# Attention in a cross-attention and mixture-of-experts block: the softmax sums and their reciprocal at the front of the pipeline step

## The chip, the core and the metric

The kernel runs on one core of a Trainium2 chip. The metric is the device time of one execution in microseconds. A core has a matrix engine (TensorE, PE in the profile), a vector engine (VectorE, DVE), an engine for activations (ScalarE, ACT), a general one (GpSimd, POOL), and queues that start transfers (SyncE, SP). Each engine works through its own instructions in order; semaphores tie the engines together. TensorE writes its results to PSUM, eight banks of 512 float32 for each of 128 partitions.

## The reference

Two parts, one after the other, on x of 2 x 2048 x 512 and a context of 2 x 128 x 512:

```
x = x + attention(layernorm(x), ctx, ctx, mask) @ W_out.T     # 16 heads of 32, 128 keys
x = x + experts(layernorm(x))                                 # 6 experts, the best 2 of each row
attention: energy = q.k, masked keys -1e20; attn = softmax(energy / sqrt(512)); out = attn.v
```

The change touches only how the softmax is divided by its sum: out = (sum over keys of exp(e) v) / (sum over keys of exp(e)).

## The kernel before

Attention is a software pipeline, written out by hand. A unit is four heads (a group g) of a block of 512 query rows: 8 blocks by 4 groups are 32 units (`ntile`). The loop `attention_loop` calls the function `attention(s)` of every engine for s = -2 to 43; step s does different stages of different units, each behind by its lag: `L_STAT` 0 (layer norm of a tile of 128 rows), `L_XT` 1 (its transposes), `L_TOK` 5 (scores by token, for the maxima), `L_MT` 9 (the maxima transposed, once for each block), `L_KEY` 10 (scores by key), `L_PV` 11 (sums, and products with the values), `L_DIV` 12 (division). What an engine does within a step is the order of the code; nothing else schedules it. All steps from 12 to 31 have every stage; step 33 and later have no tile to transpose, step 37 and later have no scores by token, the last scores by key are in step 41.

Each unit goes through these:

- Scores by token, in two pairs of heads (`scores_by_token`, pair 0 and 1; tok0 and tok1 in the prediction; the product in line 1350). Both pairs write the same two banks, `B_MX` and the next. VectorE takes the maximum over the keys (`maxima`, line 969), two reduces for each pair. Pair 1 waits for the reduces of pair 0 (`mx_done`).
- The maxima, negated and split in two by GpSimd (lines 662 and 665), are transposed by TensorE (line 1401, MT in the prediction) and copied by ScalarE (line 809).
- Scores by key (lines 1363 and 1366, "key"): four banks from `B_SC`, one for each head; the second line adds the maxima and the mask. They wait until ScalarE has read the four banks of the unit before (`exp_done`).
- ScalarE takes the four exponentials (line 785) into `prob`.
- The sums over the keys (line 1382, "den"): four matmuls with ones, into the one bank `B_DEN`. They wait for the four exponentials of the unit and for `newton_done` of the unit before, since newton is the last to read that bank.
- The reciprocal: ScalarE takes Ln of the bank (line 815) and Exp of minus that (line 817), into `rden`. VectorE multiplies the bank by it (`newton`, line 985), GpSimd makes 2 - newton of it (`less`, line 673): one Newton step.
- Products with the values (line 1411, "PV") into the bank `B_NUM`; VectorE multiplies by `rden` (`raw`, line 998), GpSimd multiplies less by raw (`atT`, line 677), and SyncE stores that to `att_d`.

Beside these TensorE transposes the normalised rows xn (line 1392, "XT"). Behind the loop follow `middle` (output projection, second layer norm, router; its first product is in line 1428, behind VectorE's split in line 1083) and `experts`.

Of the kernel before, what the change touches and what calls it, by code (L numbers as in the profile page):

```python
# [23 lines left out]
ALU = mybir.AluOpType  # L24
# [15 lines left out]
def xattn_moe(nc, x, ctx_in, mask, w_out, proj_w, anchors, routing_temp, w1, w2, out):  # L40
# [46 lines left out]
    with ctx:  # L87
# [247 lines left out]
        def live(v, n):  # L335

            return not isinstance(v, int) or 0 <= v < n
# [412 lines left out]
        def _(act):  # L750
# [26 lines left out]
                                         ACT.Copy).then_inc(s_pj, 1)  # L777

            def attention(s):
                v = s - L_KEY  # L780
                if live(v, ntile):
                    for h in range(hpg):
                        act.wait_ge(sc_ready, hpg * v + h + 1)
                        after(act, pv_done, v - 1)
                        nc.scalar.activation(prob[:, v % 2, h, :], ps[:, B_SC + h, :], ACT.Exp, scale=scale).then_inc(exp_done, 1)  # L785

                w = s - L_STAT
                if live(w, ntile):
                    n, t = w // 4, w % 4
                    act.wait_ge(rstd_done, 4 * w + 4)  # L790
                    act.wait_ge(x_in[t], 16 * (n + 1))
                    after(act, xt1_ready, w - 1)
                    nc.scalar.activation(xn[:, w % 2, :], xin[:, t, :], ACT.Identity, bias=nmr1[:, t, :],
                                         scale=rstd1[:, t, :]).then_inc(xn_done, 1)

                w = s - L_XT
                if live(w, ntile):
                    n, t = w // 4, w % 4
                    act.wait_ge(xt1_ready, w + 1)

                    after(act, sc_ready, hpg * kchunks * (n - 2))
                    nc.scalar.activation(qT[:, n % 3, :, t * P:(t + 1) * P],
                                         ps[:, B_XT, :].rearrange("p (k t) -> p k t", k=kchunks), ACT.Copy).then_inc(qT_done, 1)

                if (s - L_MT) % kchunks == 0 and live((s - L_MT) // kchunks, nblk):
                    n = (s - L_MT) // kchunks
                    act.wait_ge(mt_ready, n + 1)
                    after(act, sc_ready, hpg * kchunks * (n - 1))
                    nc.scalar.activation(mT[:, n % 2, :], ps[:, B_MT, :], ACT.Copy).then_inc(mt_done, 1)

                d = s - L_PV
                if live(d, ntile):
                    act.wait_ge(sums_ready, d + 1)
                    after(act, raw_done, d - 1)
                    nc.scalar.activation(rden[:, d % 2, :], ps[:, B_DEN, :], ACT.Ln).then_inc(den_done, 1)
                    act.wait_ge(den_done, d + 1)
                    nc.scalar.activation(rden[:, d % 2, :], rden[:, d % 2, :], ACT.Exp, scale=-1.0).then_inc(rec_done, 1)
                setup(s)

            attention_loop(attention)  # L820
# [86 lines left out]
        def _(dve):  # L907
# [65 lines left out]
            def attention(s):  # L973
                w = s - L_STAT
                if live(w, ntile):
                    n, t = w // 4, w % 4
                    dve.wait_ge(x_in[t], 16 * (n + 1))
                    after(dve, mv_done, w - 3)
                    nc.vector.bn_stats(st1[:, t, :], xin[:, t, :]).then_inc(st_done, 1)

                d = s - L_DIV
                if live(d, ntile):
                    dve.wait_ge(rec_done, d + 1)
                    after(dve, less_done, d - 1)
                    nc.vector.tensor_tensor(newton[:, d % 2, :], ps[:, B_DEN, :], rden[:, d % 2, :], ALU.mult)\
                      .then_inc(newton_done, 1)
                if live(w, ntile):
                    dve.wait_ge(st_done, w + 1)
                    after(dve, rstd_done, 4 * (w - 3))
                    nc.vector.bn_aggr(mv1[:, t, :], st1[:, t, :]).then_inc(mv_done, 1)  # L990

                v = s - L_TOK
                if live(v, ntile):
                    maxima(v, 0)
                if live(d, ntile):
                    dve.wait_ge(pv_done, d + 1)
                    after(dve, at_done, d - 1)
                    nc.vector.tensor_tensor(raw[:, d % 2, :], ps[:, B_NUM, :], rden[:, d % 2, :], ALU.mult).then_inc(raw_done, 1)
                if live(v, ntile):
                    maxima(v, 1)  # L1000
                setup(s)

            attention_loop(attention)
# [276 lines left out]
        def _(pe):  # L1280
# [86 lines left out]
                        .then_inc(sc_ready, 1)  # L1367

            def attention(s):
                k = s - L_KEY  # L1370
                if live(k, ntile):
                    scores_by_key(k)
                a = s - L_TOK
                if live(a, ntile):
                    scores_by_token(a, 0)

                v = s - L_PV
                if live(v, ntile):
                    pe.wait_ge(exp_done, hpg * (v + 1))
                    after(pe, newton_done, v)  # L1380
                    for h in range(hpg):
                        last = mm(ps[h * HD:(h + 1) * HD, B_DEN, :], ones[:], prob[:, v % 2, h, :], start=True, stop=True)  # L1382
                    last.then_inc(sums_ready, 1)

                w = s - L_XT
                if live(w, ntile):
# [175 lines left out]
```

## Time and profile before

| | |
|---|---|
| time, median of 3 runs | 766.97 us (763.25 to 771.81) |
| the profiled execution | 769.51 us, span 767.8 us |
| TensorE | busy 628.0 us, 82% of the span |
| VectorE | 454.6 us, 59% |
| ScalarE | 323.5 us, 42% |
| GpSimd | 283.0 us, 37% |
| mean granted clock of TensorE | 0.893 |

The span runs from the first to the last instruction of one execution taken by the hardware profiler. The granted clock is a share of 2.4 GHz: 1.00 is 2.4 GHz, 0.50 is 1.2 GHz. The attention loop lies in the first third of the span. A busy time of the whole span is a mean over stages with different limits, so the change has to be read from the stretch that it touches.

### The profile page before, as it was taken

The numbers are of one execution on the slowest core, as the hardware profiler recorded it, in microseconds if no ns is written. First come the engines' busy times: TensorE is split into PE (matmuls) and PEld (weight loads), VectorE is DVE, ScalarE is ACT, GpSimd is POOL, SyncE is SP. The second block draws the span as 40 slices with busy tenths as digits, with TensorE's granted clock in tenths as the row PEclk, the third lists the DMA queues.
The fourth block names the chain that finished last, engine by engine and source line by source line (L and its number), as shares of the span: only waits on it lengthen the run. The fifth ranks groups of instructions, "written<-read, shape, count | busy, mean of one in ns | idle before, by whom it ended". The sixth has DMA issues, their size and how long they took to land.

```text
span 767.8 us, 15272 instructions
## 1 busy us (share of the span) xinstructions
PE 628.0 (82%) x4628; PEld 478.9 (62%) x4629; DVE 454.6 (59%) x972; ACT 323.5 (42%) x616; POOL 283.0 (37%) x414
## 2 busy tenths in 40 slices
PE   5679999999997898899953796999999999998000
PEld 4566555555541666677742686999999888887000
DVE  3445777777654547677872363555555666766555
ACT  4225777777758156445540232333333333332000
POOL 4212555455445344767765400000000321221664
PEclk9558999999999998999975697999999999999555
DMA  5110222221411595899936625555555788887777
GB/s 171 51 42 29 84 83 85 91 93 67 152 57 70 182 319 198 300 327 309 345 158 260 220 95 194 192 193 190 183 187 191 249 283 299 263 293 238 215 252 240
DMA packets 71528, 142.91 MB, mean 186 GB/s; under 512 B 8742, under 2 KB 11814, under 8 KB 71468
## 3 DMA queue, kind: packets, MB, share of 16 engines
q1 hardware_dynamic: 61228, 108.58, 41.5%
q0 software_dynamic: 10240, 33.56, 13.3%
q8 instruction: 33, 0.54, 0.3%
q14 instruction: 27, 0.22, 0.1%
HBM read 77.63 MB, written 64.49 MB: 185 GB/s over the span
## 4 chain that ended last, share of the span: by engine, by line
PE 50%; issue 12%; DVE 12%; DMA 7%; POOL 7%; another core or an unknown queue 4%; ACT 3%; SPq 3%; DVEq 1%; POOLq 0%; ACTq 0%
PE ps L1350 8%; DMA y_d<-ysb 4%; PE ps L1363 3%; PE ps L1533 3%; PE ps L1535 3%; PE ps L1534 3%; PE ps L1512 3%; PE ps L1514 3%; PE ps L1513 3%; PE ps L1501 3%; PE ps L1411 3%; DVE nmax L969 2%; PE ps L1382 2%; PE ps L1522 2%
## 5 line engine op out<-in xcount | busy, mean ns | idle before, releaser
L724 POOL DMA_INDIRECT yg<-y_d,sidx x64 | 62.2, 972 | 258.8 <-DVE wst L1205 224.9
L969 DVE TENSOR_REDUCE nmax<-ps 128x4 f32<-128x512 f32 x128 | 82.6, 688 | 62.6 <-PE ps L1350 62.4
L1512 PE MATMUL ps<-w1H,xgH 128*128 x296 | 90.9, 307 | 3.1 <-DVE xgL L1226 3.1
L1350 PEld LDWEIGHTS ps<-kfT,qT 32*128 32x128 f32 x1024 | 72.8, 208 | 29.2 <-issue 14.2
L1350 PE MATMUL ps<-kfT,qT 32*128 32x128 f32 x1024 | 81.1, 302 | 11.2 <-DVE nmax L969 8.3
L887 ACT ACTIVATE xgH<-ps 128x512 fp32r<-128x512 f32 x74 | 44.3, 599 | 108.4 <-PE ps L1501 96.8
L785 ACT ACTIVATE prob<-ps 128x512 f32<-128x512 f32 x128 | 66.1, 602 | 48.6 <-PE ps L1366 48.6
L1514 PE MATMUL ps<-w1L,xgH 128*128 x296 | 84.6, 286 | 0.0
L1513 PE MATMUL ps<-w1H,xgL 128*128 x296 | 84.5, 286 | 0.0
L1239 DVE COPY ysb<-ps 128x512 f32<-128x512 f32 x74 | 51.0, 690 | 43.1 <-PE ps L1535 26.1
L704 POOL DMA_INDIRECT xs_d<-x,place_now x64 | 64.3, 1004 | 30.7 <-issue 20.5
L1533 PE MATMUL ps<-w2H,hH 128*128 x148 | 65.4, 442 | 0.1
L1226 DVE TENSOR_TENSOR xgL<-ps,xgH 128x512 fp32r<-128x512 f32 x74 | 51.1, 691 | 23.4 <-ACT xgH L887 17.0
L1232 DVE TENSOR_TENSOR hL<-ps,hH 128x256 fp32r<-128x256 f32 x74 | 31.3, 423 | 52.7 <-ACT hH L900 50.8
L894 ACT ACTIVATE gel<-ps 128x256 f32<-128x256 f32 x74 | 28.5, 385 | 77.7 <-PE ps L1514 62.0
L1428 PE MATMUL ps<-woH,atH 128*128 128x512 f32 x128 | 54.5, 426 | 7.3 <-DVE atL L1083 5.3
L1512 PEld LDWEIGHTS ps<-w1H,xgH 128*128 128x128 f32 x296 | 57.1, 193 | 5.3 <-issue 5.3
L1534 PE MATMUL ps<-w2H,hL 128*128 x148 | 59.2, 400 | 0.0
L1535 PE MATMUL ps<-w2L,hH 128*128 x148 | 59.1, 400 | 0.0
L1513 PEld LDWEIGHTS ps<-w1H,xgL 128*128 128x128 f32 x296 | 57.4, 194 | 0.0
L1514 PEld LDWEIGHTS ps<-w1L,xgH 128*128 128x128 f32 x296 | 57.0, 193 | 0.0
L1501 PE MATMUL ps<-ident,xg 128*128 128x128 f32 x296 | 46.5, 282 | 7.5 <-DMA xg<-xs_d 4.9
(193 smaller groups left out, 1304.7 us busy)
## 6 DMA issues: line engine op xcount, KB each, us to landing
xg<-xs_d SPq DMA_DIRECT2D x74, 256.0 KB, 3.5
y_d<-ysb SPq DMA_DIRECT2D x74, 256.0 KB
xin<-in_x SPq DMA_DIRECT2D x32, 256.0 KB, 2.7
att_d<-atT SPq DMA_DIRECT2D x32, 256.0 KB, 2.0
atL<-att_d SPq DMA_DIRECT2D x16, 512.0 KB
x<-in_x SPq DMA_DIRECT2D x32, 256.0 KB
x_d<-x SPq DMA_DIRECT2D x32, 256.0 KB
x2t<-x_d SPq DMA_DIRECT2D x16, 256.0 KB, 2.7
```

The costliest lines, as they stand in the source:

```text
L704: nc.gpsimd.indirect_dma_start(xs_d, bass.IndirectOffsetOnAxis(ap=place_now[:, n % 2, k, t:t + 1], axis=0), x2[:, n % 4, t, :], None).then ...
L724: nc.gpsimd.indirect_dma_start(yg[:, k, z, :], None, y_d[b], bass.IndirectOffsetOnAxis(ap=sidx[:, k, z:z + 1], axis=0))\
L785: nc.scalar.activation(prob[:, v % 2, h, :], ps[:, B_SC + h, :], ACT.Exp, scale=scale).then_inc(exp_done, 1)
L969: nc.vector.tensor_reduce(nmax[:, n % 2, :, g * hpg + h], ps[:, B_MX + j, :].rearrange("p (t k) -> p t k", t=4), axis=AX.X, op=ALU.max, ne ...
L1350: last = mm(ps[:, B_MX + j, t * P:(t + 1) * P], qT[r:r + HD, n % 3, g, t * P:(t + 1) * P], kfT[r:r + HD, batch_of(n), g, :], start=True, s ...
L1501: last = nc.tensor.transpose(ps[:, B_X + p, c * P:(c + 1) * P], xg[:, r, c * P:(c + 1) * P], ident[:])
L1512: mm(o, xgH[:, p, c, :], w1h[:, cols], start=(c == 0), stop=False)
L1513: mm(o, xgL[:, p, c, :], w1h[:, cols], start=False, stop=False)
L1514: last = mm(o, xgH[:, p, c, :], w1l[:, cols], start=False, stop=(c == kchunks - 1))
L1533: mm(o, hH[:, p, c, :], w2h[:, cols], start=(c == 0), stop=False)
L1534: mm(o, hL[:, p, c, :], w2h[:, cols], start=False, stop=False)
L1535: last = mm(o, hH[:, p, c, :], w2l[:, cols], start=False, stop=(c == halves - 1))
```

## The change

Three engines get another order within a step.

- TensorE: den of unit s - 11, until now between the first pair of scores by token and XT, comes first, ahead of the scores by key.
- ScalarE: Ln and Exp of the sums, until now last, come first, ahead of the exponentials.
- VectorE: newton, until now in the step after its den (lag 12) and the second operation there, comes in the step of its den (lag 11) and last.

The diff, without the lines between:

```diff
@@ ScalarE, attention(s): to the front
+                d = s - L_PV
+                if live(d, ntile):
+                    act.wait_ge(sums_ready, d + 1)
+                    after(act, raw_done, d - 1)
+                    nc.scalar.activation(rden[:, d % 2, :], ps[:, B_DEN, :], ACT.Ln).then_inc(den_done, 1)
+                    act.wait_ge(den_done, d + 1)
+                    nc.scalar.activation(rden[:, d % 2, :], rden[:, d % 2, :], ACT.Exp, scale=-1.0).then_inc(rec_done, 1)
...
@@ the same lines, behind the copy of the maxima
-                d = s - L_PV
-                if live(d, ntile):
-                    act.wait_ge(sums_ready, d + 1)
...
@@ VectorE, attention(s): behind bn_stats
                 d = s - L_DIV
-                if live(d, ntile):
-                    dve.wait_ge(rec_done, d + 1)
-                    after(dve, less_done, d - 1)
-                    nc.vector.tensor_tensor(newton[:, d % 2, :], ps[:, B_DEN, :], rden[:, d % 2, :], ALU.mult)\
-                      .then_inc(newton_done, 1)
...
                 if live(v, ntile):
                     maxima(v, 1)
+
+                u = s - L_PV
+                if live(u, ntile):
+                    dve.wait_ge(rec_done, u + 1)
+                    after(dve, less_done, u - 1)
+                    nc.vector.tensor_tensor(newton[:, u % 2, :], ps[:, B_DEN, :], rden[:, u % 2, :], ALU.mult)\
+                      .then_inc(newton_done, 1)
                 setup(s)
...
@@ TensorE, attention(s)
-                k = s - L_KEY
-                if live(k, ntile):
-                    scores_by_key(k)
-                a = s - L_TOK
-                if live(a, ntile):
-                    scores_by_token(a, 0)
-
                 v = s - L_PV
                 if live(v, ntile):
                     pe.wait_ge(exp_done, hpg * (v + 1))
...
                     last.then_inc(sums_ready, 1)
+
+                k = s - L_KEY
+                if live(k, ntile):
+                    scores_by_key(k)
+                a = s - L_TOK
+                if live(a, ntile):
+                    scores_by_token(a, 0)
```

TensorE before, in step 11 and behind it; prob,ones are the matmuls of den, qT,kT the scores by key, kfT,qT the scores by token, ident,xn the transposes:

```order
L1363 MATMUL ps<-qT,kT 128x512 [waits mt_done,qT_done,exp_done]
L1363 MATMUL ps<-qT,kT 128x512 x3
L1366 MATMUL ps<-mT,selT 128x512 x4
L1350 MATMUL ps<-kfT,qT 128x128 [waits mx_done,s_kfT,qT_done]
L1350 MATMUL ps<-kfT,qT 128x128 x7
L1382 MATMUL ps<-prob,ones 32x512 [waits exp_done]
L1382 MATMUL ps<-prob,ones 32x512 x3
L1392 MATMUL ps<-ident,xn 128x128 [waits exp_done,qT_done,xn_done]
```

The same step of TensorE after the change (its lines are numbered by the new file):

```order
L1378 MATMUL ps<-prob,ones 32x512 [waits exp_done]
L1378 MATMUL ps<-prob,ones 32x512 x3
L1366 MATMUL ps<-qT,kT 128x512 [waits mt_done,qT_done,exp_done]
L1366 MATMUL ps<-qT,kT 128x512 x3
L1369 MATMUL ps<-mT,selT 128x512 x4
L1353 MATMUL ps<-kfT,qT 128x128 [waits mx_done,s_kfT,qT_done]
L1353 MATMUL ps<-kfT,qT 128x128 x7
L1395 MATMUL ps<-ident,xn 128x128 [waits exp_done,qT_done,xn_done]
```

The four matmuls of den went from behind the first pair of scores by token to the head of the step. From step 12 on the first of them waits for newton_done as well, before and after.

VectorE before, one step from its statistics to the next:

```order
L979 BN_STATS st_90<-xin 128x6 [waits mv_done,x_in1]
L985 TENSOR_TENSOR newton<-ps,rden 128x512 [waits less_done,rec_done]
L990 BN_AGGR mv_91<-st_90 128x2 [waits rstd_done,st_done]
L969 TENSOR_REDUCE nmax<-ps 128x4 [waits nml_done,mx_ready] x2
L998 TENSOR_TENSOR raw<-ps,rden 128x512 [waits at_done,pv_done]
L969 TENSOR_REDUCE nmax<-ps 128x4 [waits nml_done,mx_ready] x2
L979 BN_STATS st_90<-xin 128x6 [waits mv_done,x_in2]
```

VectorE after the change, the same step:

```order
L980 BN_STATS st_90<-xin 128x6 [waits mv_done,x_in1]
L986 BN_AGGR mv_91<-st_90 128x2 [waits rstd_done,st_done]
L970 TENSOR_REDUCE nmax<-ps 128x4 [waits nml_done,mx_ready] x2
L994 TENSOR_TENSOR raw<-ps,rden 128x512 [waits at_done,pv_done]
L970 TENSOR_REDUCE nmax<-ps 128x4 [waits nml_done,mx_ready] x2
L1002 TENSOR_TENSOR newton<-ps,rden 128x512 [waits less_done,rec_done]
L980 BN_STATS st_90<-xin 128x6 [waits mv_done,x_in2]
```

Newton went from behind the statistics to behind the second pair of reduces, and is now that of the unit whose den is in the same step.

## Rows read from the trace of the kernel before

In the timeline a row gives the start and the length in us, the engine, the line of the code, the operation, what it writes and reads, how often, and in brackets the idle time of the engine ahead of it with what ended it. In the table of stretches a row gives the stretch, its length, the busy time (and the number of instructions) of PE, PEld (TensorE's weight loads), DVE, ACT and POOL, the granted clock, the share of the DMA engines and GB/s.

**Rows 1.** Table of stretches: attention, its last steps, and a part of these.

```profile
61.00:224.30 163.30, 159.61 (x1733) 90.31 (x1729) 115.57 (x204) 115.14 (x211) 77.96 (x150) 0.99 0.24 82
224.30:252.10 27.80, 18.82 (x164) 5.66 (x160) 12.70 (x17) 19.53 (x35) 14.90 (x16) 0.99 0.19 72
...
245.00:250.00 5.00, 1.84 (x16) 0.36 (x15) 3.04 (x5) 3.12 (x4) 3.58 (x4) 1.00 0.14 52
```

**Rows 2.** Timeline of TensorE's matmuls, step 26 and the start of step 27.

```profile
159.40 1.14 PE L1363 MATMUL ps<-qT,kT 32*128 32x512 f32 x8
...
160.59 1.06 PE L1350 MATMUL ps<-kfT,qT 32*128 32x128 f32 x16
161.58 1.06 PE L1382 MATMUL ps<-prob,ones 128*32 128x512 f32 x8
162.58 0.66 PE L1392 MATMUL ps<-ident,xn 128*128 128x128 f32 x4
163.16 1.16 PE L1350 MATMUL ps<-kfT,qT 32*128 32x128 f32 x16
164.25 1.07 PE L1411 MATMUL ps<-prob,ctok 128*32 128x512 f32 x8
165.25 0.71 PE L1363 MATMUL ps<-qT,kT 32*128 32x512 f32 x4
```

**Rows 3.** Timeline of TensorE: scores by key of steps 11, 12, 13, 14, 37; MT.

```profile
67.19 1.09 PE L1363 MATMUL ps<-qT,kT 32*128 32x512 f32 x5
...
73.69 1.14 PE L1363 MATMUL ps<-qT,kT 32*128 32x512 f32 x8
...
79.55 1.14 PE L1363 MATMUL ps<-qT,kT 32*128 32x512 f32 x8
...
83.67 0.66 PE L1401 MATMUL ps<-ident,nmhl 128*128 128x128 f32 x4 [0.29 <-POOL nmhl L665]
...
86.34 1.14 PE L1363 MATMUL ps<-qT,kT 32*128 32x512 f32 x8
...
224.29 1.14 PE L1363 MATMUL ps<-qT,kT 32*128 32x512 f32 x8
```

**Rows 4.** Timeline of VectorE in step 26: its reduces, then the next statistics.

```profile
161.68 1.29 DVE L969 TENSOR_REDUCE nmax<-ps 128x4 f32<-128x512 f32 x2 [0.61 <-PE ps L1350]
...
164.36 1.29 DVE L969 TENSOR_REDUCE nmax<-ps 128x4 f32<-128x512 f32 x2 [0.79 <-PE ps L1350]
165.56 0.68 DVE L979 BATCH_NORM_STATS2 st<-xin 128x6 f32<-128x512 f32 x1
```

**Rows 5.** Timeline of TensorE in step 36: the two pairs of scores by token.

```profile
219.78 1.06 PE L1350 MATMUL ps<-kfT,qT 32*128 32x128 f32 x16
...
222.21 1.16 PE L1350 MATMUL ps<-kfT,qT 32*128 32x128 f32 x16 [0.37 <-DVE nmax L969]
```

**Rows 6.** Timeline of steps 40 and 41: exponentials, key, newton, den.

```profile
237.18 2.06 ACT L785 ACTIVATE prob<-ps 128x512 f32<-128x512 f32 x4 [0.47 <-PE ps L1366]
...
239.44 1.14 PE L1363 MATMUL ps<-qT,kT 32*128 32x512 f32 x8
...
240.43 0.69 DVE L985 TENSOR_TENSOR newton<-ps,rden 128x512 f32<-128x512 f32 x1 [2.39 <-ACT rden L817]
...
241.27 1.06 PE L1382 MATMUL ps<-prob,ones 128*32 128x512 f32 x8 [0.45 <-DVE newton L985]
```

**Rows 7.** Timeline of ScalarE in step 26: the exponentials.

```profile
160.78 2.07 ACT L785 ACTIVATE prob<-ps 128x512 f32<-128x512 f32 x4 [1.62 <-PE ps L1366]
```

**Rows 8.** Timeline: last den, its Ln, the first product of the next stage.

```profile
244.92 1.07 PE L1382 MATMUL ps<-prob,ones 128*32 128x512 f32 x8 [1.73 <-DVE newton L985]
...
246.04 0.60 ACT L815 ACTIVATE rden<-ps 128x512 f32<-128x512 f32 x1 [1.99 <-PE ps L1382]
...
252.15 0.77 PE L1428 MATMUL ps<-woH,atH 128*128 128x512 f32 x1 [5.31 <-DVE atL L1083]
```

**Rows 9.** Timeline of TensorE ahead of the first key, granted clock 0.50.

```profile
52.29 2.08 PE L1350 MATMUL ps<-kfT,qT 32*128 32x128 f32 x16 [0.30 <-DVE nmax L969]
```

More of the change, by code:

```diff
@@ L809, in attention @@
                     nc.scalar.activation(mT[:, n % 2, :], ps[:, B_MT, :], ACT.Copy).then_inc(mt_done, 1)
-                d = s - L_PV
-                if live(d, ntile):
-                    act.wait_ge(sums_ready, d + 1)
[L814 to L817, printed above, removed]
                 setup(s)
```

## The prediction

> **What bounds the kernel now.** I read the table of stretches first, since the change touches only the attention stage. From 61.0 us (the first scores by key) to 224.3 us TensorE is busy 159.6 of 163.3 us at a granted clock of 0.99; from there to 252.1 us it is busy 18.8 of 27.8 us [rows 1]. So for most of attention the end of a step is set by TensorE itself. The timeline of one step shows that there is no hole to close [rows 2]: scores by key at 159.40, the first pair of scores by token (tok0) at 160.59, the sums (den) at 161.58, the transposes of xn (XT) at 162.58, the second pair (tok1) at 163.16, the products with the values (PV) at 164.25, the next key at 165.25. Each group starts where the one before stops streaming; the step is 5.85 us. The steps in which the maxima are transposed as well (MT at 83.67, one step in four) take 6.79 us, as 79.55 to 86.34. From the key of step 12 at 73.69 to that of step 37 at 224.29 there are 25 steps [rows 3]: 150.6 us, 6.02 on the mean.
>
> Then VectorE in the same step [rows 4]. Its two reduces of tok0 run from 161.68 to 162.97, and tok1 starts at 163.16: both pairs share the two banks at B_MX, and tok1 waits for these reduces. Here den and XT cover the wait exactly. The reduces of tok1 run from 164.36 to 165.65, past the end of PV; nobody waits for them, since tok0 of the next step is more than a microsecond away. In steps 34 to 36, which have no XT, the cover is too short and the wait is seen: 0.37 us of idle time ahead of tok1, with 2.43 us from tok0 to tok1 [rows 5]. That is the interval whenever the reduces set it.
>
> From step 37 on there are no scores by token, and ScalarE's exponentials set the pace: they run from 237.18 to 239.24, and the next key starts at 239.44 [rows 6]. Steps 37 to 40 take 15.15 us (224.29 to 239.44). Ln and Exp of the sums come behind the exponentials, beside the next key, and cost nothing.
>
> **What the change does.** No operation is added or dropped, and each keeps the waits that it had; only places move.
>
> (a) On TensorE den moves from between tok0 and XT to the front of the step. Between tok0 and tok1 only XT is left: tok1 could start 1.0 + 0.58 = 1.57 us after tok0 (the spacings of [rows 2] without den). The reduces of tok0 ask for 2.43 [rows 5]. New idle time: 0.86 us a step.
>
> (b) On VectorE newton of unit v moves from the step after to the end of the step of den of v, behind the reduces of tok1. Den of unit v+1 overwrites the one bank at B_DEN, so it waits for newton of v, and it is now the first thing that TensorE does in the next step. The chain: from tok1 1.20 us to the start of its reduces (163.16 to 164.36), 1.20 from there to VectorE's next operation (164.36 to 165.56) [rows 2, 4], newton 0.69, and 0.15 from its end to den, as 240.43 + 0.69 to 241.27 [rows 6]. That is 3.23 us from tok1 to den. TensorE has work for 2.09 of it (tok1 1.09, PV 1.0). New idle time: 1.14 us a step. In TensorE's queue key, tok0 and all the rest stand behind den, and VectorE's reduces wait for these: the ring closes, and nothing catches the loss up.
>
> A full step is then den to key 1.0 (as PV to key), key to tok0 1.20, tok0 to tok1 2.43, tok1 to the next den 3.23: **7.86 us**. MT lies between XT and tok1 and takes 0.59 there; due 1.57 after tok0, it fits into the idle 0.86 if its operand is ready. That operand comes from GpSimd behind the mean and variance, and today it sets MT's start (0.29 us of idle time, 4.12 after key [rows 3]). The statistics start 0.31 after key now [rows 2, 4] and would start as newton ends, 0.2 ahead of den, and newton no longer stands between their two halves: 1.1 us earlier against the step's start. So the operand is ready 3.0 us after den and MT is due at 3.8. Steps with MT are 7.86 too. 25 steps are 196.5 us: 45.9 more than 150.6.
>
> (c) On ScalarE Ln and Exp stand ahead of the exponentials. Ln starts 1.12 us after den (244.92 to 246.04) and takes 0.60 to 0.63 [rows 8]; I take Exp as long, so they end some 2.4 us after den. The scores are there 1.38 after key (159.40 to 160.78 [rows 2, 7]), which is 2.38 after den. The exponentials are delayed by less than 0.1 and end at 4.5 of 7.86; ScalarE is busy 115.1 us in the whole stretch [rows 1], under 5 us a step, so the full steps hide it. In steps 37 to 40 nothing does: den waits for all four exponentials of the step before, 2.45 us to their start, 2.07 for them, 0.2 to TensorE [rows 6]: 4.72 us. Four such steps are 18.9 us against 15.15: 3.7 more.
>
> (d) The ends. Step 11, the first with den, has 6.50 us (67.19 to 73.69 [rows 3]) and gets the new ring: 1.4 more. From the key of step 41 at 239.44 to the first product of the next stage at 252.15 there are 12.7 us. After the change, counted from den of step 41: den of step 42 at 4.72, Ln at 1.12 behind it, and from Ln to that product 6.1 as now (246.04 to 252.15 [rows 8]): 11.9. So 0.8 less.
>
> Sum: 45.9 + 3.7 + 1.4 - 0.8 = **+50.2 us**. The profiled execution has a span of 767.8 us and a time of 769.5; these become 818 and 820. It lies 2.5 us above the median of the three runs, 767.0, so for a median I say **817 us**.
>
> Not in the sum: GpSimd's less and atT and the stores of att_d. Less finds newton done a step early, atT waits for raw as now, and both have a step of 7.86 us to hide in; the last atT lies beside the splits of the next stage. 0 for all; a half microsecond once if the last one collides otherwise.
>
> **The clock.** The idle time would cost more than itself if the granted clock fell. In the rows it is 0.99 over 224.3 to 252.1, where TensorE is busy two thirds of the time, and holds at 1.00 through 245 to 250 with 1.84 us busy of 5 [rows 1]. The new step is busy 5.85 of 7.86, in holes of about 1 us. I take no loss. The Trainium skill, TensorE: Matmul & The Clock Gate, section "A second HAM failure mode: psum-queue depth-cycling", says that TensorE idling briefly and often between groups of matmuls as it cycles through PSUM buffers can make the clock swing between its two levels. By that rule the new step, which stops for a PSUM bank twice, is in danger; the rows just named speak against it.
>
> **Rivals.**
> *Only one of the two waits stands.* If VectorE freed B_MX in time for tok1, the step were 1.0 + 1.20 + 1.57 + 3.23 = 7.00, with the same ends +28: 795. If newton did not hold den, 1.0 + 1.20 + 2.43 + 2.09 = 6.72 and +21: 788. Against it: the first wait is seen today without den's help [rows 5], and the reduces of tok1 end 0.3 us behind PV before newton has begun [rows 2, 4]. 8 in 100.
> *Not slower.* Newton and the reduces hide behind TensorE after all. One mechanism would do it: VectorE's tail behind tok1 (1.20 + 1.20 + 0.69 + 0.15) shrinking below TensorE's 2.09 us, which needs 1.14 us less a step. Five steps with MT would then hide their 0.93 us, the ends cost 3, and it comes to 765. For it speaks that VectorE idles in every step; but it idles ahead of the reduces, waiting for TensorE, and not behind them. 3 in 100.
> *The clock falls to 1.2 GHz within attention.* At 0.50 the sixteen matmuls of tok0 take 2.08 us in place of 1.06 [rows 9, 2]; with TensorE's parts of the ring doubled (2.0 + 2.4 + 3.4 + 4.2) a step is 12.0 us: over 900 if it lasted, 840 to 870 for a part. 3 in 100.
> *A third link joins the ring.* XT needs the first exponential, done some 3.0 us after den, where XT is due at 3.2; behind it there are 0.86 us to spare, so only a delay above 1 us would show. Half a microsecond in each step is +12: 830 to 835. 4 in 100.
>
> **The numbers.** My forecast has 82 in 100. Its own uncertainty: 0.2 us in each of 25 steps (how fast den and tok1 start after a wait, whether MT hides) is 5 us, the time at which the clock rises ahead of step 12 some 2, the spread of the three runs (763.3 to 771.8) 4: 805 to 829. The rivals below hold 11 in 100, those above 7, and no more than 20 are to be left out, so the range stays. About 1% is what a measurement of this kernel can tell from no change. Faster by more than that: 1 in 100; within it: 3; slower: 96.
>
> **What would show it.** Den's matmuls are the first group of a step and carry about 1.1 us of idle time put down to newton; tok1 carries about 0.8 put down to the reduces; from den to den 7.9 us with MT or without; clock 1.00 from 75 to 270 us; 4.7 us in the last steps, their exponentials right behind Exp; the stages behind attention as long as before. I am wrong if den starts directly behind PV, or if a step is above 8.3 us, which would mean a link that I have not seen.

## The result and the profile after

The changed kernel takes 824.64 us (median of 4 runs, 821.32 to 830.10) against 766.69 (4 runs, 763.25 to 771.81): 1.076 times as long, 95% interval 1.067 to 1.084. The forecast was 817, range 805 to 829. The profiled execution has a span of 823.2 us, 55.4 above before, where the sum said 50.2.

The table of stretches, which answers to [rows 1] (columns as there). The first stretch is steps 12 to 35, the second goes from step 37 to the first product of the next stage:

```profile
76.92:271.51 194.59, 155.43 (x1548) 83.27 (x1549) 106.05 (x184) 106.11 (x191) 73.48 (x141) 0.93 0.20 67
...
279.71:309.98 30.27, 19.18 (x160) 5.10 (x161) 12.04 (x15) 20.07 (x35) 14.28 (x15) 1.00 0.16 61
```

TensorE was busy nearly all the time in this stage and is now busy four fifths of it, and the granted clock, which was 0.99, is 0.93. One step of it, the timeline of step 25 with MT (den at 180.72, key, tok0, XT, MT, tok1, PV), then VectorE's reduces and newton of the step before, answering to [rows 2] to [rows 5]:

```profile
180.72 1.06 PE L1378 MATMUL ps<-prob,ones 128*32 128x512 f32 x8 [1.07 <-DVE newton L1002]
181.71 1.14 PE L1366 MATMUL ps<-qT,kT 32*128 32x512 f32 x8
182.91 1.05 PE L1353 MATMUL ps<-kfT,qT 32*128 32x128 f32 x16
183.90 0.66 PE L1395 MATMUL ps<-ident,xn 128*128 128x128 f32 x4
184.39 0.60 PE L1404 MATMUL ps<-ident,nmhl 128*128 128x128 f32 x4
185.35 1.16 PE L1353 MATMUL ps<-kfT,qT 32*128 32x128 f32 x16 [0.36 <-DVE nmax L970]
186.44 1.06 PE L1414 MATMUL ps<-prob,ctok 128*32 128x512 f32 x8
```

```profile
177.49 1.16 PE L1353 MATMUL ps<-kfT,qT 32*128 32x128 f32 x16 [0.79 <-DVE nmax L970]
178.68 1.29 DVE L970 TENSOR_REDUCE nmax<-ps 128x4 f32<-128x512 f32 x2 [0.65 <-PE ps L1353]
179.89 0.68 DVE L1002 TENSOR_TENSOR newton<-ps,rden 128x512 f32<-128x512 f32 x1
```

Both new waits stand where the prediction put them. Den waits 1.07 us for newton, and newton stands behind the second pair of reduces; tok1 waits 0.79 us for the first pair of reduces, 0.36 in a step with MT, since MT fills part of the hole. From tok1 to den it is 3.23 us (177.49 to 180.72), from den to den 7.85, with MT and without (180.72 to 188.57).

Where the 57.9 us of attention lie (first product of the next stage at 310.01 against 252.15): 0.2 ahead of step 11; 3.0 in step 11 (9.50 us against 6.50); 52.2 in the 25 steps from 12 to 36 (76.92 to 279.71, 202.8 us against 150.6); 3.4 in steps 37 to 40 (18.56 against 15.15); the end gives back 1.0 (11.74 against 12.71). The rest of the kernel is 2.4 us shorter (513.2 against 515.6), where nothing was changed; I take it for scatter between executions. The 25 steps are 196.3 us at 7.85 and 6.5 us more, in single steps of 7.9 to 8.5 and one of 11.6. The long one is step 35 (den at 259.92), with tok1 of step 34 ahead of it; a small one is step 15. Timeline of TensorE:

```profile
256.69 1.16 PE L1353 MATMUL ps<-kfT,qT 32*128 32x128 f32 x16 [1.37 <-DVE nmax L970]
...
259.92 1.94 PE L1378 MATMUL ps<-prob,ones 128*32 128x512 f32 x8 [0.96 <-DVE newton L1002]
261.78 2.09 PE L1366 MATMUL ps<-qT,kT 32*128 32x512 f32 x8
...
267.37 2.08 PE L1353 MATMUL ps<-kfT,qT 32*128 32x128 f32 x16 [1.38 <-DVE nmax L970]
```

```profile
100.56 1.55 PE L1378 MATMUL ps<-prob,ones 128*32 128x512 f32 x8 [0.19 <-DVE newton L1002]
102.04 1.14 PE L1366 MATMUL ps<-qT,kT 32*128 32x512 f32 x8
```

The matmuls take twice as long (den 1.94 for 1.06): the clock was at 1.2 GHz for these. In the small case it is back at 2.4 GHz before key, and the wait for newton has shrunk from 1.07 to 0.19 us: the idle time of the step before took part of the loss, so only what goes beyond it is seen in the step. The long fall comes where the hole is longest: step 34 is the first without transposes and without MT, and its tok1 waits 1.37 us in place of 0.79. In a second profile of the changed kernel (after_again below) the only long step, 11.59 us, is step 35 as well.

The last steps, the timeline of step 39, answering to [rows 6]: den, Ln, Exp, the exponentials, the next den.

```profile
289.25 1.06 PE L1378 MATMUL ps<-prob,ones 128*32 128x512 f32 x8 [1.14 <-ACT prob L793]
290.38 0.60 ACT L784 ACTIVATE rden<-ps 128x512 f32<-128x512 f32 x1 [1.19 <-PE ps L1378]
291.01 0.63 ACT L786 ACTIVATE rden<-rden 128x512 f32<-128x512 f32 x1
291.64 2.06 ACT L793 ACTIVATE prob<-ps 128x512 f32<-128x512 f32 x4
293.76 1.07 PE L1378 MATMUL ps<-prob,ones 128*32 128x512 f32 x8 [1.14 <-ACT prob L793]
```

### The profile page after: what moved, and what is told of

It is laid out like the page before. It is cut to its first block, busy times and chain, and to the rows that moved or that the text cites. A ratio compares the mean times of both kernels' runs of the same rounds, so it can differ in the third digit from the quotient of the medians.

```text
span 823.2 us, 15272 instructions
## 1 busy us (share of the span) xinstructions
PE 643.6 (78%) x4628; PEld 482.3 (59%) x4629; DVE 456.0 (55%) x972; ACT 325.7 (40%) x616; POOL 283.5 (34%) x414
## 4 chain that ended last, share of the span: by engine, by line
PE 48%; issue 15%; DVE 15%; DMA 7%; POOL 4%; SPq 4%; ACT 3%; another core or an unknown queue 2%; DVEq 1%; POOLq 0%; ACTq 0%
PE ps L1353 10%; DVE nmax L970 6%; PE ps L1378 5%; PE ps L1366 4%; DMA y_d<-ysb 4%; PE ps L1536 3%; PE ps L1538 3%; PE ps L1537 3%; PE ps L1515 3%; PE ps L1516 3%; PE ps L1517 3%; PE ps L1504 3%; DVE newton L1002 2%; PE ps L1431 1%
## 5 line engine op out<-in xcount | busy, mean ns | idle before, releaser
L1353 PE MATMUL ps<-kfT,qT 32*128 32x128 f32 x1024 | 83.0, 307 | 29.4 <-DVE nmax L970 26.5
L1353 PEld LDWEIGHTS ps<-kfT,qT 32*128 32x128 f32 x1024 | 74.6, 213 | 47.2 <-DVE nmax L970 29.7
L677 POOL TENSOR_TENSOR atT<-less,raw 128x512 f32<-128x512 f32 x32 | 41.6, 1300 | 79.0 <-issue 72.9
L1378 PE MATMUL ps<-prob,ones 128*32 128x512 f32 x256 | 38.3, 671 | 28.0 <-DVE newton L1002 23.4
L784 ACT ACTIVATE rden<-ps 128x512 f32<-128x512 f32 x32 | 19.1, 597 | 102.9 <-PE ps L1378 102.9
L895 ACT ACTIVATE gel<-ps 128x256 f32<-128x256 f32 x74 | 28.5, 385 | 75.5 <-PE ps L1517 58.3
```

Source lines behind the costliest of these rows:

```text
L1353: last = mm(ps[:, B_MX + j, t * P:(t + 1) * P], qT[r:r + HD, n % 3, g, t * P:(t + 1) * P], kfT[r:r + HD, batch_of(n), g, :], start=True, s ...
```

## The experiments

The theory: the loss is a ring of two waits (B_MX ahead of tok1, newton ahead of den) that den's new place closes, 7.85 us a step, and on top of it a granted clock that falls now and then because TensorE idles. The rivals: newton's or ScalarE's new place costs by itself; the clock falls for a reason of its own. The runs were made in four sessions. The kernel before took 770.7 us in the first (median of 19), 755.0 in the second (7), 754.0 in the third (25) and 753.0 in the fourth (13), so a time is compared only within its session, and steps are compared by the profiles: they are the same to 0.02 us in all sessions at the same clock.

### Newton alone

The kernel before, with only this move on VectorE:

```diff
-                if live(d, ntile):            # newton of unit s - 12, behind bn_stats
-                    dve.wait_ge(rec_done, d + 1)
...
                     maxima(v, 1)
+                u = s - L_PV                  # newton of unit s - 11, last
+                if live(u, ntile):
+                    dve.wait_ge(rec_done, u + 1)
...
```

> The kernel before with VectorE's newton alone moved to the end of the step of its den; TensorE and ScalarE keep their old order. Theory (the loss is the ring that closes because den is now FIRST on TensorE): newton ends about 1.1 us behind PV, but den of the next step comes 2.2 us into it, so nobody waits: steps of 5.85 and 6.79 us, 767 us. Rival (newton behind the reduces costs by itself, through GpSimd's less and atT or through VectorE's later statistics): steps above 6 us, 770 to 785.

769.93 us (10 runs) against 770.66: ratio 1.001 (0.996 to 1.005). Newton stands behind the reduces as in the changed kernel, and the steps are 5.85 us:

```profile
94.45 1.29 DVE L969 TENSOR_REDUCE nmax<-ps 128x4 f32<-128x512 f32 x2 [0.79 <-PE ps L1352]
95.65 0.68 DVE L1001 TENSOR_TENSOR newton<-ps,rden 128x512 f32<-128x512 f32 x1
```

Newton's place costs nothing as long as den comes late in TensorE's step. Only the steps with MT grew, from 6.79 to 6.92 us: the statistics now start behind newton, and GpSimd's operand for MT is later with them. I had expected 6.79 there too.

### Newton back, ScalarE back

Two runs that each undo one part of the change. In the first newton is again behind the statistics of the next step, with den still first:

```diff
                     nc.vector.bn_stats(st1[:, t, :], xin[:, t, :]).then_inc(st_done, 1)
                 d = s - L_DIV
+                if live(d, ntile):
+                    dve.wait_ge(rec_done, d + 1)
...
-                u = s - L_PV
-                if live(u, ntile):
...
```

> The changed kernel with VectorE's part undone: newton behind the statistics of the next step again, den still first on TensorE. Theory that den waits for newton, whatever stands ahead of newton on VectorE: the statistics (0.60 us from start to start) join the chain, 8.45 us a step in steps 12 to 32 and 7.85 in 33 to 36, 21 steps by 0.6 = 12.6 us more: 833 to 841 with the clock's dips. Rival that newton's new place is the fault: the time falls back toward 767 to 800.

841.37 us (4 runs, 835.94 to 848.92) against 809.12 for the changed kernel in the same session (the run after_again below). The undisturbed step is 8.44 us, as the theory said, with the statistics in the chain (8.45 expected):

```profile
95.73 1.06 PE L1376 MATMUL ps<-prob,ones 128*32 128x512 f32 x8 [1.66 <-DVE newton L986]
...
104.17 1.06 PE L1376 MATMUL ps<-prob,ones 128*32 128x512 f32 x8 [1.66 <-DVE newton L986]
```

The 0.59 us more of den's wait, in the 19 steps from 12 to 30, explain 11 us. The attention stage of the two profiles differs by 26.5 us (268.8 against 242.3 from den of step 11 to the first product), and most of what remains is the clock: eleven of these steps take 10.0 to 10.5 us, and over steps 12 to 31 the granted clock is 0.81:

```profile
76.93:265.90 188.97, 151.51 (x1301) 74.06 (x1301) 88.36 (x158) 91.94 (x165) 65.15 (x131) 0.81 0.16 52
```

I had expected about 13 us more than the changed kernel, and some 30 came: the clock's part was larger than foreseen.

In the second ScalarE's Ln and Exp are last in the step again:

```diff
             def attention(s):
-                d = s - L_PV
-                if live(d, ntile):
-                    act.wait_ge(sums_ready, d + 1)
...
                     nc.scalar.activation(mT[:, n % 2, :], ps[:, B_MT, :], ACT.Copy).then_inc(mt_done, 1)
+                d = s - L_PV
+                if live(d, ntile):
+                    act.wait_ge(sums_ready, d + 1)
...
```

> The changed kernel with ScalarE's part undone: Ln and Exp of the sums last in the step again, TensorE and VectorE as changed. Theory: in the full steps the ring den, key, tok0, tok1, reduces, newton sets the pace and the reciprocal is ready at about the time at which the reduces end, so 7.85 us stays, a few tenths more in steps with the copy of the maxima (8.2); in the last steps den waits for newton, which waits for Exp behind the four exponentials: 1.0 + 1.38 + 2.07 + 1.3 + 0.7 + 0.15 = 6.6 us a step in place of 4.5. Together some 8 to 12 us above the changed kernel: 832 to 837. Rival that Ln and Exp at the front are what costs: the time falls by more than 5 us, below 820.

823.37 us (4 runs) against 809.12: 14 us more, where 8 to 12 were expected. The full steps stay at 7.85, those with the copy of the maxima 8.13. Of the last steps the first without MT takes 6.48 us, near the 6.6 expected, and then the clock falls there too, so that the next take 8.0 to 8.5: timeline of step 39 (its den, then newton) and the start of 40.

```profile
291.44 1.93 PE L1378 MATMUL ps<-prob,ones 128*32 128x512 f32 x8 [3.11 <-DVE newton L1002]
...
298.60 0.69 DVE L1002 TENSOR_TENSOR newton<-ps,rden 128x512 f32<-128x512 f32 x1 [6.71 <-ACT rden L818]
299.44 1.93 PE L1378 MATMUL ps<-prob,ones 128*32 128x512 f32 x8 [3.11 <-DVE newton L1002]
```

So neither of these two moves is the fault: with den first, both are the better places.

### One wait taken away, then the other

Newton goes ahead of the second pair of reduces, into time in which VectorE is idle:

```diff
+                u = s - L_PV
+                if live(u, ntile):
+                    dve.wait_ge(rec_done, u + 1)
...
                 if live(v, ntile):
                     maxima(v, 1)
-
-                u = s - L_PV
...
```

> The changed kernel with newton ahead of the second pair of reduces instead of behind it (VectorE is idle there; the reciprocal is ready 2.4 us after den). Den keeps its place at the head of the step. Theory of two separate waits: the wait for newton goes, the wait for B_MX ahead of tok1 stays: 1.0 + 1.20 + 2.43 + 2.09 = 6.72 us a step, 25 steps 17 us above before, with the last steps as in the changed kernel: about 790. If only one wait was real, 5.9 a step (770) or 7.85 (825). On the clock: if the dips of the changed kernel come from TensorE's idle time, 0.86 us idle in 6.72 should give fewer of them than 2.0 in 7.86, or none.

797.26 us (4 runs) against 770.66: 1.038 (1.026 to 1.050). The step is 6.58 us (94.80 to 101.38), with 0.80 us of idle time ahead of tok1 and none ahead of den:

```profile
99.40 1.16 PE L1352 MATMUL ps<-kfT,qT 32*128 32x128 f32 x16 [0.80 <-DVE nmax L970]
99.86 0.68 DVE L999 TENSOR_TENSOR newton<-ps,rden 128x512 f32<-128x512 f32 x1
100.49 1.06 PE L1413 MATMUL ps<-prob,ctok 128*32 128x512 f32 x8
...
101.38 1.04 PE L1377 MATMUL ps<-prob,ones 128*32 128x512 f32 x8
```

The wait for newton is one of the two, worth 1.27 us a step. I had expected 6.72: den follows PV 0.89 us later, not 1.0. And I had expected 790; the clock is the difference. That expectation failed: with the shorter holes the clock still fell four times in the 25 steps, and nine steps together lost 9.7 us, 4.8 of it in steps 34 to 36, where tok1 waits 1.37 us.

Then PV goes between XT and tok1 as well, with raw ahead of the first reduces:

```diff
+                if live(v, ntile):            # PV
+                    b, g = batch_of(unit(v)[0]), unit(v)[1]
+                    after(pe, raw_done, v)
...
                 if live(a, ntile):
                     scores_by_token(a, 1)
-                if live(v, ntile):
...
```

> As e2_newton_early, and PV on TensorE moved between XT and tok1, with raw on VectorE ahead of the first pair of reduces so that PV finds its bank free. Theory: PV covers what den covered before, so B_MX's wait goes too: steps 5.86 to 5.9 us, MT steps at or under 6.5 since GpSimd's operand is early; what is left of the change is the last steps, 4.5 us against 3.7, and the start: 766 to 771. Rival (den at the head costs beyond the two waits, say through the exponentials behind Ln and Exp): steps above 6.2, over 775. On the clock: no dips between 75 and 225 us.

775.54 us (10 runs) against 770.66: 1.009 (1.005 to 1.013). The plain step is 5.85 us, the same as before the change, with den still at the head; the clock is 1.00 throughout. So the whole of the ring was these two waits. What I missed are the steps with MT, 7.32 us and not 6.5:

```profile
80.24 0.68 DVE L980 BATCH_NORM_STATS2 st<-xin 128x6 f32<-128x512 f32 x1
...
83.17 0.35 POOL L665 TENSOR_TENSOR nmhl<-nmax,nmhl 128x64 fp32r<-128x64 f32 x1
...
83.58 0.66 PE L1404 MATMUL ps<-ident,nmhl 128*128 128x128 f32 x4 [0.81 <-POOL nmhl L665]
```

When den does not wait for the reduces, these run on past den, and the statistics, the mean and GpSimd's operand come that much later: MT waits 0.81 us. Five such steps, 2.7 us, and the last steps as in the changed kernel, 3.4 us, less the 1.0 that the end gives back, make the 5 us. The expected range ended at 771, so this expectation of the time failed, by the steps with MT; the rival's time, over 775, came, but not its steps above 6.2.

### The clock: the holes filled

The changed kernel with added matmuls whose results are never used. In the first only the hole ahead of den is filled, in the second also that ahead of tok1 (not in the steps with MT):

```diff
                     last.then_inc(pv_done, 1)
+                if live(a, ntile) and live(k, ntile):
+                    pe.wait_ge(exp_done, hpg * (k + 1))
+                    for j in range(2):
+                        mm(ps[:, B_SC + 2 + j, 0:256], ident[:], xn[:, w % 2, 0:256], start=True, stop=True)
...
+                if live(a, ntile) and live(k, ntile) and (s - L_MT) % kchunks:     # second kernel only, ahead of tok1
+                    pe.wait_ge(exp_done, hpg * k + 2)
+                    mm(ps[:, B_SC + 1, 0:384], ident[:], xn[:, w % 2, 0:384], start=True, stop=True)
```

> The changed kernel with two added matmuls behind PV in steps 10 to 36 (128 x 128 by 256 columns into the banks of the scores, whose contents are overwritten later and not used), 0.85 us of the 1.14 us in which TensorE waits for newton. The ring is not touched: steps stay 7.85. Theory that TensorE's idle time makes the granted clock dip: no or fewer steps above 7.9 between 77 and 272 us and clock 1.00 there, some 4 to 8 us less than the changed kernel: 817 to 821. Rival that the dips have another source (they come at some places in time whatever TensorE does): as many dips, 824; if the added work stands in the ring's way, more.

> As e6_fill, with one more added matmul (384 columns, 0.64 us) in the idle time ahead of tok1, except in the steps with MT, into a bank whose contents are overwritten later and not used. TensorE is then busy some 7.5 of 7.85 us. Theory that idle time makes the clock dip: none between 77 and 272 us (e6_fill, with one of the two holes filled, had two and a half, the changed kernel five), steps 7.85 to 7.9, 4 to 7 us less than the changed kernel of the same session. Rival: as many dips as the changed kernel in the same session, whose dips then have nothing to do with idle time.

> The changed kernel once more, for a second profiled execution and beside e9_fill_both on the same chip. Theory: the ring is the same to 0.02 us (7.85), the dips of the clock come at other places and in another number, three to seven of them costing 0.4 to 1 us each, now and then one of ten microseconds that costs 4: 820 to 832.

The second kernel (e9_fill_both) does what the theory said of the ring and of the clock. Timeline of a step of it; L1423 and L1409 are the added matmuls:

```profile
110.73 1.07 PE L1378 MATMUL ps<-prob,ones 128*32 128x512 f32 x8
...
114.40 0.81 PE L1409 MATMUL ps<-xn,ident 128*128 128x384 f32 x2
115.36 1.16 PE L1353 MATMUL ps<-kfT,qT 32*128 32x128 f32 x16
116.44 1.07 PE L1417 MATMUL ps<-prob,ctok 128*32 128x512 f32 x8
117.44 1.13 PE L1423 MATMUL ps<-xn,ident 128*128 128x256 f32 x4
118.58 0.64 PE L1378 MATMUL ps<-prob,ones 128*32 128x512 f32 x4
```

From step 11 to step 36 all 26 steps take 7.85 us. The tables of stretches from step 12 to the end of step 35 (the last into step 36): the changed kernel a second time, the first hole filled, both filled.

```profile
79.23:273.70 194.47, 155.50 (x1548) 83.35 (x1549) 106.01 (x184) 106.03 (x191) 73.31 (x141) 0.93 0.20 67
```

```profile
78.62:270.07 191.45, 173.40 (x1644) 97.93 (x1645) 106.07 (x184) 106.20 (x191) 74.00 (x141) 0.98 0.20 68
```

```profile
79.33:271.98 192.65, 186.50 (x1718) 103.88 (x1718) 106.99 (x186) 109.16 (x197) 73.94 (x141) 1.00 0.20 68
```

Beyond 7.85 us a step, the 25 steps lost 6.5 us in the changed kernel, 6.4 in its second profile, 4.0 with one hole filled and nothing with both; step 11 took 9.50, 9.32, 8.74 and 7.86. The two kernels with added work have one profile each. By the time, in the second session, both filled 805.23 us (4 runs, 798.45 to 807.88) and the changed kernel 809.12 (806.53 to 812.10). The 4 us fit the expectation, but the two ranges overlap, and the time alone would not settle it. The mean granted clock of whole executions does not overlap: 0.905 to 0.911 in the four with both holes filled, 0.887 to 0.895 in the four of the changed kernel. The attention stage of the profiles differs by 7.9 (234.4 against 242.3 from den of step 11 to the first product); den of step 11 came 1.6 us later with the added work (71.47 against 69.91), and the stages behind attention took 3.4 us more in this pair of executions. Why was not tried. With only one hole filled nothing is to be seen in the time (826.23 us where before took 770.66, ratio 1.075, 1.066 to 1.084): that expectation of the time failed. In its profile the steps from 12 to 36 lost 2.5 us less than in the changed kernel's, but den of step 11 came 2.5 us later (69.88 against 67.42).

### From the clock to a faster kernel

Two findings apply to the kernel before. MT waits for GpSimd there, and TensorE runs at 0.50 from 24 to 64 us, into step 10 (the second stretch below is full steps of scores by token, 6.97 us each), with holes of 0.3 and 1.5 us in its steps. The kernel before, table of stretches:

```profile
24.00:40.00 16.00, 12.05 (x83) 9.80 (x83) 7.77 (x15) 4.97 (x8) 3.66 (x12) 0.50 0.15 45
40.00:56.00 16.00, 11.01 (x80) 8.96 (x77) 8.50 (x16) 2.90 (x5) 2.42 (x8) 0.50 0.16 50
```

First GpSimd's two operations on the maxima, moved ahead of its statistics:

```diff
             def attention(s):
+                if (s - L_MT) % kchunks == 0 and live((s - L_MT) // kchunks, nblk):
+                    n = (s - L_MT) // kchunks
+                    pool.wait_ge(mx_done, HEADS * (n + 1))
...
                 w = s - L_STAT
                 if live(w, ntile):
...
```

> The kernel before with one move on GpSimd: in the steps with MT the two operations on the maxima come ahead of the statistics, since the maxima of the last step are already there. In before MT waits for them 0.3 us and starts 4.12 us after key. Theory: MT starts right behind XT, steps with MT take 6.79 - 0.37 = 6.42 us, five or six of them: 2 us less, below what the times can tell, but to be read in the profile. Rival: xn's bias comes 0.8 us later and delays XT of the next step; then nothing is won.

751.75 us (10 runs) against 754.03: 0.997 (0.993 to 1.001), not to be told from no change by the time. In the profile five steps with MT take 6.29 us in place of 6.79 and MT starts right behind XT:

```profile
82.72 0.66 PE L1392 MATMUL ps<-ident,xn 128*128 128x128 f32 x4
83.21 0.60 PE L1401 MATMUL ps<-ident,nmhl 128*128 128x128 f32 x4
83.74 1.16 PE L1350 MATMUL ps<-kfT,qT 32*128 32x128 f32 x16
```

Then matmuls of the unit matrix in steps 1 to 9 of the kernel before, and both together:

```diff
+            def idle(n):
+                pe.wait_ge(s_kT, batches)
+                for j in range(n):
+                    mm(ps[:, B_DEN, (j % 4) * P:(j % 4 + 1) * P], ident[:], ident[:], start=True, stop=True)
...
+                if 5 <= s <= 9:
+                    idle(2)
                 if live(a, ntile):
                     scores_by_token(a, 1)
+                if 1 <= s <= 9:
+                    idle(4 if s >= 5 else 8)
```

> The kernel before with added matmuls (128 x 128 by 128 columns of the unit matrix, into the bank of the sums, not used) in steps 1 to 9, where TensorE is idle between the scores by token and the granted clock is 0.50 from 24 to 64 us. Theory from the dips (idle time of TensorE lowers the clock): with the idle time filled the clock is 1.00 before step 10, the steps 5 to 9 take about 5 us in place of 6.97, the first key comes 6 to 12 us earlier: 757 to 763. Rival: the clock stays at 0.50 since the added work is itself too thin, and as it stands in the queue ahead of the scores at half the clock it costs: 770 to 780.

> Both of the former: the added matmuls of e8_warm and the maxima ahead of the statistics on GpSimd. If each works as said the two add, 8 to 14 us below before: 755 to 761.

With the added matmuls alone (e8_warm) 755.99 us (10 runs) against 754.03, ratio 1.002 (0.998 to 1.007): nothing won, although the clock was 1.00 from 40 to 66 us in its profile. The profile shows where the gain went: the work added in steps 1 to 4 put the first scores by token at 30.83 us in place of 27.94, MT of step 9 waited 1.36 us for GpSimd, and step 10, which has no added work, was followed by a fall to 0.50, so that step 11 took 9.04 us in place of 6.50. Key of step 12 stands at 75.37 us, in the kernel before at 73.69. With both (e10_warm_maxima) 11 runs fell into two groups, six of 743.4 to 746.5 us at a mean granted clock of 0.926 to 0.932 and five of 756.2 to 760.9 us at 0.903 to 0.909, so one median does not describe it. Its profile is of the upper group: from 40 to 66 us the clock was 0.50, with TensorE without any idle time. The tables of e8_warm and e10_warm_maxima:

```profile
24.00:40.00 16.00, 11.69 (x92) 10.40 (x92) 5.78 (x11) 5.46 (x9) 3.51 (x17) 0.79 0.19 50
40.00:56.00 16.00, 13.32 (x146) 11.63 (x146) 11.26 (x22) 4.08 (x7) 3.61 (x12) 1.00 0.18 51
```

```profile
24.00:40.00 16.00, 12.95 (x90) 11.74 (x92) 6.30 (x12) 5.08 (x9) 2.68 (x11) 0.70 0.18 50
40.00:56.00 16.00, 16.00 (x102) 14.20 (x100) 7.37 (x15) 2.90 (x5) 3.34 (x11) 0.50 0.14 34
```

The last kernel keeps GpSimd's move, and in steps 5 to 10 has three added matmuls of 256 columns of the context. (Its expectation counts those of e10_warm_maxima by records of the profile, two for each matmul: in the code they are six a step and eight in steps 1 to 4. Six of 128 columns and three of 256 are the same 768 columns.)

```diff
-                for j in range(n):
-                    mm(ps[:, B_DEN, (j % 4) * P:(j % 4 + 1) * P], ident[:], ident[:], start=True, stop=True)
+                for j in range(n // 2):
+                    mm(ps[:, B_DEN, j * 2 * P:(j + 1) * 2 * P], ident[:], ctok[:, 0, 0:2 * P], start=True, stop=True)
...
-                if 1 <= s <= 9:
-                    idle(4 if s >= 5 else 8)
+                if 5 <= s <= 10:      # behind tok1; idle(2) ahead of it, in the same steps
+                    idle(4)
```

> As e10_warm_maxima, but the added matmuls stand only in steps 5 to 10 (three of 256 columns of the context a step, where e10 had twelve of 128 columns of the unit matrix, and sixteen in steps 1 to 4 that delayed the transposes by up to 3 us). In the profile of e10 the clock stayed at 0.50 from 31 to 66 us although the records show TensorE without idle time, while e8 was at 1.00 from 40 to 66. Theory that what counts is how much of the array the work uses, and not only idle time: wider moving operands raise the clock in step 6 or 7 each time, steps 7 to 9 take 5.1 us in place of 6.97, the first key comes 3 to 6 us earlier, all executions in one group: 746 to 750 where before is 754 (in the other kind of session 14 us more for both). Rival: two groups again, or the clock at 0.50 until 60 us, and then 752 to 758.

747.40 us (8 runs, 744.28 to 748.89, one group) against 752.99 (13 runs): 0.990 (0.987 to 0.994). All eight executions lie below all thirteen of the kernel before; it is the one kernel of the study of which that can be said, and it leaves nothing of the work out. How much of it is the added work and how much GpSimd's move the times do not separate.

```profile
24.00:40.00 16.00, 12.97 (x75) 10.58 (x76) 7.02 (x14) 4.16 (x7) 2.44 (x8) 0.54 0.20 51
40.00:56.00 16.00, 13.68 (x133) 10.46 (x133) 10.86 (x21) 4.08 (x7) 5.23 (x17) 1.00 0.17 51
56.00:66.00 10.00, 9.65 (x95) 6.81 (x95) 6.00 (x11) 5.04 (x10) 1.76 (x7) 1.00 0.18 52
```

The clock rises in step 6, at about 38 us, with TensorE busy less than in e10_warm_maxima; the first key comes at 58.8 us, step 10 has added work too, and step 11 stays at 1.00 and takes 5.86 us, where it took 9.04 in e8_warm, without work in step 10. The next stage starts at 246.4 us, against 249.7 with GpSimd's move alone. Whether the wider moving operand, the data or the place of the added work made the clock rise here and not in e10_warm_maxima was not separated, so the expectation's theory of how much of the array the work uses is not shown, though its times came.

## Why the prediction was right, and where it was not

**The ring (parts a and b): right.** 7.86 us a step was forecast, 7.85 came, with both waits and their sizes (0.86 and 1.14 forecast; 0.79 and 1.07 of idle time in the rows, which count from the end of the group before). Taking one wait away left 6.58, taking both away 5.85, adding the statistics to the chain 8.44. That MT hides was right too: GpSimd's operand ended 3.05 us after den (180.72 to 183.77), 3.0 forecast.

**The step that failed: "I take no loss" for the clock.** The rows of before at a low busy share and a clock of 1.00 (245 to 250 us) were short stretches; over 200 us of steps with holes the clock fell five times, and once more at step 11. It cost 6.5 us in the 25 steps and 1.6 in step 11: 8 of the 55. With these 8 the sum comes to 58.3, against 57.9 in the attention stage; that the whole was 55.4, and so nearer to the 50.2 forecast, is the 2.4 us of scatter behind it. A warning stood in the trace of before: from 24 to 56 us it has holes in each step, TensorE is busy 23.06 of 32 us, and the granted clock is 0.50 (rows in the last experiments). The prediction used [rows 9] for the price of a slow matmul and did not ask why the clock was low there. The rule of the Trainium skill (TensorE: Matmul & The Clock Gate, section "A second HAM failure mode: psum-queue depth-cycling") named just this danger, and the runs bear it out: 0.93 with both holes, 0.98 with one filled, 1.00 with both filled. I had made it a rival of 3 in 100 priced from 840 us on. The runs make it a term of the likeliest case, some 8 us, and not a rival: the dips are mostly short, and in this ring the idle time that causes them also takes up part of their cost.

**The ends (parts c and d): mis-sized, small.** A last step takes 4.50 us, not 4.72: den follows the exponentials 0.06 us after their end (291.64 + 2.06 to 293.76), where I had taken the 0.2 from the exponentials to key, and these start 2.39 us after den, not 2.45. Step 37 still has MT and takes 5.06. Steps 37 to 40 cost 3.4 and not 3.7, the end gives back 1.0 and not 0.8. Step 11 was forecast 1.4 longer and is 3.0 longer; 1.6 of that is the clock.

**The rivals.** "Only one of the two waits stands" and "not slower" are excluded by the rows. "The clock falls" came in small: four falls cost 0.6 to 0.7 us each, the one at step 11 1.6 and the long one 4.1, not 20 and more. "A third link" did not show in the changed kernel, but it is there once the ring is open: in e3_pv_between GpSimd's operand held MT.

## What to carry to other kernels

Before an operation is moved to the front of an engine's step, look at what its old place covered (here the wait for a bank between two halves of the scores) and at who must have read its output buffer by then: with one buffer, moving the producer ahead and its last reader back closes a ring, though no wait was added. Such a ring is summed from a row for each link, and came out to 0.01 us; what has to be added for a TensorE that was full and now has holes in each step is the clock, which only long stretches of a trace show; stretches of the old kernel that already have such holes are the place to look. Where TensorE idles for another reason, filling it with work that is not used can be worth more than it costs, but it has to delay nothing, and by these runs it has to reach up to the full steps: of the fillings of the start, the one that delayed the first scores and left step 10 out (e8_warm) won nothing.

## What the hardware showed that I had not expected

- Holes of 0.8 us in each 6.58 us step (1.37 in steps 34 to 36) were enough for the clock to fall four times in 174 us (e2_newton_early), and the visible loss, 9.7 us, was larger than with twice the idle time (6.5 us), where the granted clock was about the same (0.93 against 0.94 over the 25 steps): with long holes half-speed matmuls run into idle time, with short ones into the next step.
- TensorE stayed at 0.50 for over 30 us without idle time in the records (e10_warm_maxima, 16.00 us busy of 16 in the stretch shown), and rose to 1.00 in e11_warm_later at a lower busy share.
- The same kernel took 771 us in one session and 753 to 755 in others, with the same steps in attention at the same clock. In the profiles the difference lies behind attention: from its first product to the end 513.2 to 516.8 us in all of the result and of the first session, 496.1 to 499.5 in all later ones, whatever was done to attention. Why is not known.
